# Half of each norm on VectorE, ranks from logits, a last sum by halves, and orders of smaller pieces in a small vision tower with a mixture of experts

## The reference

```
h = tok(x)
h = h + A(norm(h))     linear attention, elu features
h = h + B(norm(h))     softmax attention, qkv with 2 of 8 low-rank experts
h = h + C(norm(h))     attention with normed q and k, softmax over the queries; + its input
h = h + D(norm(h))     norm, softmax attention and a gelu MLP; second half of the batch with smaller branches
h = h + E(norm(h))     attention with a polynomial in place of exp
h = h + F(norm(h))     one int8 product
h = h + G(norm(h))     softmax attention, then a norm with gain and bias (G2)
h = h + H(norm(h))     2 of 8 experts (192 -> 768 gelu -> 192) by a softmax gate
```

## Time and profile before

| | us |
|---|---|
| median of three runs | 493.92 |
| lowest, highest of them | 493.78, 496.96 |
| the profiled execution, its time | 493.1 |
| its span, first to last instruction | 491.0 |
| TensorE busy | 434.6 |
| VectorE busy | 281.4 |
| ScalarE busy | 170.9 |
| GpSimd busy | 122.5 |

### The profile page before, as it was taken

How to read it: one execution, slowest core, us unless ns; L and a number is a source line. 1 busy time by engine, 2 the same in 40 slices (tenths; PEclk the granted TensorE clock), 3 DMA queues, 4 the chain that set the end, 5 groups by cost and what they waited for, 6 DMA issues and landing times.

```text
span 491.0 us, 11691 instructions
## 1 busy us (share of the span) xinstructions
PE 434.6 (89%) x4616; PEld 381.4 (78%) x4616; DVE 281.4 (57%) x862; ACT 170.9 (35%) x460; POOL 122.5 (25%) x169
## 2 busy tenths in 40 slices
PE   4999879999889889998999998989899779999990
PEld 4966767978578778787887887878889668999990
DVE  2367825858558894686346557698988451313111
ACT  0231022406051423553456431346332016354430
POOL 8120620102112003302021202430022175532230
PEclk9999959999999989999999998999998769999996
DMA  8647200000025000000000800101383113998003
GB/s 329 151 100 195 60 0 2 4 1 1 1 64 155 1 1 1 2 3 1 1 1 1 287 6 1 65 1 54 108 265 74 39 57 103 308 328 283 27 24 127
DMA packets 26320, 39.76 MB, mean 81 GB/s; under 512 B 5612, under 2 KB 17916, under 8 KB 26268
## 3 DMA queue, kind: packets, MB, share of 16 engines
q1 hardware_dynamic: 24348, 34.99, 23.4%
q0 software_dynamic: 1632, 3.34, 2.2%
q10 hardware_dynamic: 288, 0.70, 0.4%
HBM read 35.43 MB, written 3.59 MB: 79 GB/s over the span
## 4 chain that ended last, share of the span: by engine, by line
PE 58%; DVE 16%; SPq 9%; issue 5%; POOL 4%; ACT 4%; DMA 3%; POOLq 0%; DVEq 0%
PE bank L1574 8%; PE bank L1668 8%; PE bank L1691 7%; PE bank L1621 6%; PE bank L1918 3%; PE bank L1626 3%; PE bank L1930 3%; PE bank L1866 3%; PE bank L1583 2%; SPq L511 2%; ACT xn L809 2%; PE bank L1903 2%; PE bank L1639 2%; DVE stats L1019 2%; POOL rstd L670 1%
## 5 line engine op out<-in xcount | busy, mean ns | idle before, releaser
L1574 PE MATMUL bank<-constants 128*128 128x128 f32 x622 | 83.8, 287 | 0.0
L1574 PEld LDWEIGHTS bank<-constants 128*128 128x128 f32 x622 | 76.5, 199 | 4.9 <-issue 4.1
L670 POOL TENSOR_TENSOR rstd<-rstd_tmp,minus_half 101x4 f32<-101x4 f32 x20 | 20.3, 1016 | 198.3 <-DVE rstd_tmp L1029 198.2
L809 ACT ACTIVATE xn<-h,minus_mean_rstd,rstd 101x192 f32<-101x192 f32 x64 | 30.0, 559 | 40.8 <-POOL minus_mean_rstd L677 40.7
L1918 PEld LDWEIGHTS bank<-vblk,et 101*64 101x64 f32 (+1 forms) x960 | 29.4, 127 | 4.4 <-issue 4.2
L1918 PE MATMUL bank<-vblk,et 101*64 101x34 f32 (+1 forms) x960 | 30.4, 220 | 2.3 <-ACT et L937 2.1
L1621 PE MATMUL bank<-weights,nT 128*101 128x192 f32 (+2 forms) x128 | 28.7, 366 | 0.9 <-DVE vblk L1083 0.9
L790 POOL DMA_INDIRECT rows_y<-et,out_row x17 | 17.0, 1002 | 43.8 <-DVE et L1529 42.4
L1621 PEld LDWEIGHTS bank<-weights,nT 128*101 128x101 f32 x128 | 19.6, 175 | 6.6 <-issue 6.5
L1709 PE MATMUL bank<-weights,scores 128*101 128x192 f32 x96 | 18.4, 362 | 6.9 <-DMA scores<-in_patches 6.9
L1903 PEld LDWEIGHTS bank<-packing,scores 101*101 101x101 f32 x240 | 22.2, 169 | 2.1 <-issue 2.1
(11 more groups left out here) (343 smaller groups left out, 933.1 us busy)
## 6 DMA issues: line engine op xcount, KB each, us to landing
weights<-in_w SPq DMA_DIRECT2D x7, 576.0 KB, 4.9
weights<-in_w SPq DMA_DIRECT2D x7, 384.0 KB, 5.0
scores<-in_patches SPq DMA_DIRECT2D x4, 606.0 KB, 7.1
scores<-in_w SPq DMA_DIRECT2D x4, 576.0 KB, 6.2
...
```

The costliest lines, as they stand in the source:

```text
L670: link(g.tensor_tensor(rstd[0:ROWS, a], rtmp[0:ROWS, a], mhalf[0:ROWS, a], ALU.pow))
L809: ins = sc.activation(dst, src, ACT.Identity, scale=rstd[0:ROWS, r:r + 1], bias=nmr[0:ROWS, r:r + 1])
L1574: mm(PS[b][:, 0:128], ident, ident, start=True, stop=True)
```

## The change

- Norms: ScalarE normalises rows 2 and 3 of an oct's four, VectorE rows 0 and 1, at the start of its step T (or G2), as soon as the power is there (`root_ready`); it uses mean and root directly, so it doesn't wait for GpSimd's product. Whoever reads the result waits for both (`normalised`). `moments` signals the variance first and the mean after it (`mean_ready`); two of the four aggregations are made ahead of the second two pairs' statistics.
- H's gate: ranks are made from the logits, ahead of the maximum, with one comparison against a constant triangle of 0 and a tiny number in place of two.
- Last sum: both loads, the additions and the store go by two halves of the columns; SP stores the first, ScalarE's queue the second.
- Orders: phases may be cut into pieces (PE_PARTS, DVE_PARTS, ACT_PARTS), and the order strings go over the pieces. All four strings are new, and so is IDLE, with 297 fillers in place of 319. In A's O the products of the two groups are no longer interleaved, attention's O waits for half of the values and transposes only, and C's key statistics are aggregated piece by piece.

```diff
-IDLE = {('A', 'T', 0): 6, ('A', 'M', 0): 7, ('A', 'M', 0, 1): 3, ('A', 'O', 0): 1, ('A', 'M', 1): 1, ('A', 'M', 1, 1): 3, ('A', 'O', 1): 1, ('A', 'Z', 1): 9, ('B', 'T', 0): 1, ('B', 'G', 0): 1, ('B', 'H', 0, 1): 1, ('B', 'F', 0): 5, ('B', 'S', 0): 14, ('B', 'H', 1, 1): 1, ('B', 'P', 0): 1, ('B', 'S', 1): 14, ('B', 'Z', 1): 8, ('C', 'S', 0): 6, ('C', 'T', 1): 1, ('C', 'R', 1): 32, ('C', 'S', 1): 6, ('C', 'Z', 0): 1, ('C', 'P', 0): 1, ('C', 'O', 1): 16, ('C', 'Z', 1): 1, ('C', 'P', 1): 1, ('D', 'T', 0): 9, ('D', 'F', 0): 1, ('D', 'S', 0): 8, ('D', 'F', 1): 3, ('D', 'P', 0): 1, ('D', 'O', 1): 2, ('D2', 'P', 0): 2, ('D2', 'U', 1): 1, ('E', 'S', 0): 8, ('E', 'P', 0): 1, ('E', 'O', 1): 4, ('E', 'P', 1): 1, ('G', 'T', 0): 16, ('F', 'T', 1): 7, ('G', 'S', 0): 9, ('G', 'T', 1): 7, ('G', 'F', 1): 2, ('G', 'O', 1): 22, ('H', 'T', 0): 9, ('H', 'G', 0): 2, ('H', 'C', 0): 12, ('H', 'T', 1): 30, ('H', 'G', 1): 1, ('H', 'C', 1): 11, ('rows',): 8}
+IDLE = {('A', 'T', 0): 2, ('A', 'M', 0): 7, ('A', 'M', 0, 1): 3, ('A', 'T', 1): 2, ('A', 'Z', 0): 2, ('A', 'O', 1, 1): 5, ('B', 'H', 0, 1): 1, ('B', 'F', 0): 5, ('B', 'T', 1): 1, ('B', 'S', 0): 6, ('C', 'K', 0): 1, ('B', 'P', 1): 13, ('C', 'R', 0): 2, ('C', 'S', 0): 6, ('C', 'R', 1): 34, ('C', 'P', 0): 14, ('C', 'Z', 1): 1, ('C', 'P', 1): 1, ('D', 'T', 0): 8, ('D', 'F', 0): 1, ('D', 'S', 0): 8, ('D', 'S', 1): 7, ('D', 'Z', 1): 3, ('D2', 'P', 1): 3, ('E', 'F', 0): 1, ('E', 'T', 1): 4, ('E', 'F', 1): 1, ('E', 'Z', 1): 3, ('G', 'T', 0): 25, ('F', 'T', 1): 2, ('G', 'S', 0): 14, ('G', 'F', 1): 2, ('G', 'S', 1): 20, ('G', 'O', 1, 1): 15, ('H', 'G', 0): 1, ('H', 'C', 0): 13, ('H', 'T', 1): 44, ('H', 'G', 1): 1, ('H', 'C', 1): 7, ('rows',): 8}
...
-ORDER_PE = ("0100010101011001000100101001101101110001001111110001110000110101001101010011101001001010011010110101001101011011000111")
-ORDER_DVE = ("0100010101011000100101001001101011101001011011010110110001001100110100110101101001001100011011010101010101011010010111")
-ORDER_ACT = ("1000101010001100101000011010001111110001100110101101101010010100110101100110011010011100011000110101100100110100011111")
-ORDER_POOL = ("0100101000110010110011101000110011010110001010001100111100100010101110101010110001001001111011011010101011000001111011")
-
-
-def schedule(order):
-
-    steps, at = [], [0, 0]
+ORDER_PE = ("0011000000101101110101001010100100001010111111001100001000110011011101101111000101001001001101011110101010101100110010000100110101111010010100111000000111110110100111")
+ORDER_DVE = ("000101000010011011001011010011100100010100101000001101110010101111100001010001010000100011110101001011011111111011111001010100100100011011101100000101110011101001111010001101011010001011100001010010010111010110101001010101010100100110011001010010010111110101101111")
+ORDER_ACT = ("0010010010110100010111001011000100000000110101111111011010100001000010011010101011010011111111110001100000100001011111000111110101001001001111100111010000111001001000011111100100011011010100010100000101111011101010101111")
+ORDER_POOL = ("0100110100000100111001111001111000010011000100110110101100111010011001001101010001100111010101011001011011000101011101")
+
+
+PE_PARTS = {"tok": 2, "M": 2, "X": 4, "O": 2, "V": 2}
+DVE_PARTS = {'tok': 2, 'A.F': 2, 'M': 2, 'F': 2, 'S': 4, 'W': 2, 'X': 4, 'N': 4, 'O': 2, 'K': 4, 'R': 2, 'V': 2, 'P': 2, 'T': 2, 'F.T': 2}
+ACT_PARTS = {"T": 2, "A.F": 2, "S": 4, "X": 4, "O": 2, "R": 3, "U": 4}
+POOL_PARTS = {}
...
+def schedule(order, parts):
+
+    steps, at, whole = [], [0, 0], []
+    for n, ph in PHASES:
+        k = parts.get(n + "." + ph, parts.get(n if n == "tok" else ph, 1))
+        whole += [(n, ph, i, k) for i in range(k)]
     for q in map(int, order):
-        steps.append(PHASES[at[q]] + (q,))
+        steps.append(whole[at[q]] + (q,))
         at[q] += 1
-    assert at == [len(PHASES)] * 2
-    assert [q for n, p, q in steps if (n, p) == ("H", "C")] == [0, 1]
+    assert at == [len(whole)] * 2
+    assert [q for n, p, i, k, q in steps if (n, p) == ("H", "C")] == [0, 1]
     return steps
 
 
-PE_STEPS, DVE_STEPS, ACT_STEPS, POOL_STEPS = map(schedule, (ORDER_PE, ORDER_DVE, ORDER_ACT, ORDER_POOL))
+def section(items, i, k):
+
+    return items[len(items) * i // k:len(items) * (i + 1) // k]
...
+        halves = [slice(FLAT // 2 * x, FLAT // 2 * x + FLAT // 2) for x in range(2)]
...
+        mean_ready = Signal(sem("mean_ready"), [e for e in norms_by(DVE_STEPS) if e[0] != "Cqk"])
+        root_ready = Signal(sem("root_ready"), [e for e in norms_by(POOL_STEPS) if e[0] != "Cqk"])
         rstd_ready = Signal(sem("rstd_ready"), norms_by(POOL_STEPS))
-        xn_ready = Signal(sem("xn_ready"), norms)
+        xn_ready, xn_begun = Signal(sem("xn_ready"), norms(ACT_STEPS)), Signal(sem("xn_begun"), norms(DVE_STEPS))
...
+        def normalised(eng, n, q):
+
+            eng.wait_ge(*xn_begun.at((n, q)))
+            eng.wait_ge(*xn_ready.at((n, q)))
...
-            sp.dma_start(choice[0], flat_rows(rows_y[0:T])).then_inc(choice_loaded[0], 16)
+            for x in range(2):
+                sp.dma_start(choice[0][:, halves[x]], flat_rows(rows_y[0:T])[:, halves[x]]).then_inc(choice_loaded[0][x], 16)
             sp.wait_ge(summed, 2)
-            sp.dma_start(flat_rows(out), total_h).then_inc(stored, 16)
-            sp.wait_ge(stored, 16)
+            sp.dma_start(flat_rows(out)[:, halves[0]], total_h[:, halves[0]]).then_inc(stored, 16)
+            sp.wait_ge(stored, 32)
...
-                link(g.tensor_tensor(rstd[0:ROWS, a], rtmp[0:ROWS, a], mhalf[0:ROWS, a], ALU.pow))
+                root_of = g.tensor_tensor(rstd[0:ROWS, a], rtmp[0:ROWS, a], mhalf[0:ROWS, a], ALU.pow)
                 if n == "D":
 
+                    link(root_of)
                     link(g.tensor_tensor(rtmp[0:ROWS, a], mv[0:ROWS, a, 1], rstd[0:ROWS, a], ALU.mult))
                     link(g.tensor_tensor(rtmp[0:ROWS, a], rtmp[0:ROWS, a], rstd[0:ROWS, a], ALU.mult))
                     link(g.tensor_scalar(rtmp[0:ROWS, a], rtmp[0:ROWS, a], EPS, None, ALU.add))
-                    link(g.tensor_tensor(rst2[0:ROWS, a], rtmp[0:ROWS, a], mhalf[0:ROWS, a], ALU.pow))
+                    root_of = g.tensor_tensor(rst2[0:ROWS, a], rtmp[0:ROWS, a], mhalf[0:ROWS, a], ALU.pow)
+                root_of.then_inc(*root_ready.inc((n, q)))
+                pool.wait_ge(*root_ready.at((n, q)))
+                pool.wait_ge(*mean_ready.at((n, q)))
...
-                for p in range(P8):
+                for p in range(BY_DVE, P8):
...
-            act.dma_start(choice[1], rows_y[T:2 * T].rearrange("t d -> (t d)").rearrange("(a b) -> a b", a=128)).then_inc(choice_loaded[1], 16)
+            for x in range(2):
+                act.dma_start(choice[1][:, halves[x]],
+                              rows_y[T:2 * T].rearrange("t d -> (t d)").rearrange("(a b) -> a b", a=128)[:, halves[x]]).then_inc(choice_loaded[1][x], 16)
+            act.wait_ge(summed, 4)
+            act.dma_start(out.rearrange("t d -> (t d)").rearrange("(a b) -> a b", a=128)[:, halves[1]], total_h[:, halves[1]]).then_inc(stored, 16)
...
+                if c % 2:
+                    settle()
+                    aggregate(c - 1)
...
-                for p in range(P8 * q, P8 * q + P8):
-                    mark(v.bn_aggr(mv[0:ROWS, p], stats[0:ROWS, p]))
+                aggregate(2 * q + 1)
                 settle()
                 a = slice(P8 * q, P8 * q + P8)
-                mark(v.tensor_scalar(nmr[0:ROWS, a], mv[0:ROWS, a, 0], -1.0, None, ALU.mult))
                 v.tensor_scalar(rtmp[0:ROWS, a], mv[0:ROWS, a, 1], EPS, None, ALU.add).then_inc(*var_ready.inc((n, q)))
+                v.tensor_scalar(nmr[0:ROWS, a], mv[0:ROWS, a, 0], -1.0, None, ALU.mult).then_inc(*mean_ready.inc((n, q)))
...
+            def normalise(n, q):
+
+                dve.wait_ge(*root_ready.at((n, q)))
+                for p in range(BY_DVE):
+                    r = P8 * q + p
+                    src, dst = (yt[q][0:ROWS, p], x2[q][0:ROWS, p]) if n in ("D2", "G2") else (h[0:ROWS, r], xn[0:ROWS, r])
+                    ins = v.tensor_scalar(dst, src, mv[0:ROWS, r, 0:1], rstd[0:ROWS, r:r + 1], ALU.subtract, ALU.mult)
+                    if n == "D" or p < BY_DVE - 1:
+                        mark(ins)
+                if n == "D":
+                    settle()
+                    for p in range(BY_DVE):
+                        r = P8 * q + p
+                        ins = v.tensor_scalar(x2[q][0:ROWS, p], xn[0:ROWS, r], rst2[0:ROWS, r:r + 1], None, ALU.mult)
+                        if p < BY_DVE - 1:
+                            mark(ins)
+                ins.then_inc(*xn_begun.inc((n, q)))
...
+                if n == "H":
+                    whose = ahead_by[0:ROWS].rearrange("p (i j) -> p i j", j=NE).unsqueeze(1).broadcast_to([ROWS, P8, NE, NE])
+                    link(v.tensor_tensor(diff, lg.unsqueeze(2).broadcast_to([ROWS, P8, NE, NE]),
```

(49 more changed lines are left out.)

201 lines of the change are left out of this document (111 added, 90 removed).

## The result

Median of 20 runs each: 492.41 us (488.12 to 496.63) against 496.75 us (493.78 to 503.18) before, 4.3 us less. The ratio, which leaves out slow executions (those over 1.5% longer than the fastest of their kernel), is 0.993, 95% interval 0.9901 to 0.9959; by it the change is worth 3.5 us. The forecast was 485.3 for 493.92, a ratio of 0.983. The sign was right and the time lies in the range, but of the 8.6 us forecast only 3.5 came.

The account below looks back on a forecast made before the run. No one engine bounds the whole; TensorE does in D, VectorE from G to H. Terms -5.9 + 3.8 + 0 - 1.4 + 0.8 - 5.9 = -8.6 us on 493.1 give 484.5, as a median 485.3; range 475 to 495.

Parts of the forecast that it names:

- VectorE's rows cost nothing at D2: At D2 of oct 0, as at B0, VectorE idles, so its half of the norm adds no time: 0.
- three pairs: VectorE's two-row norm pieces from F to H, where it is the bound: six at 0.63 us, +3.8 us in all.
- Part 1: All norms, half on VectorE: eight norms on the chain gain 0.74 us each, -5.9; VectorE's own queue pays +3.8.
- the 0.2 us for meeting GpSimd: At each chain norm, VectorE's and GpSimd's work stretch each other: 0.2 us taken off the 0.94 gain.
- the port rival: Four of VectorE's new pairs meet a GpSimd row addition and lose 1.5 us each: 491.3 us, chance 0.06.
- VectorE's wait for the power: At six norms in B to E VectorE waits about 10 us for GpSimd's power, costed at nothing because it idles there.
- Part 2: H's ranks from logits: oct 1's norm behind routing +2.3, given back by copy, picks and filler; sum 0, ends -1 and +1.5.
- the walk: Stepping through the four new order strings with the timelines' durations, leaving out contention and hand-over jitter; its moves make -8.8 us.
- Part 3: Last sum by halves at the kernel's end: additions -1.0 and smaller last store -0.4, together -1.4 us.
- Part 4: New orders in A to E: A +0.8; B -0.5, C -2.0, D0 -2.9, D2 -2.1, E -1.3, these five taken at two thirds, -5.9.
- Clock: Rival: 10 us more work at the 1.2 GHz level, half of that time lost, some 4.5: 489.8 us, chance 0.09.
- orders give nothing: Rival: VectorE stays the bound and TensorE's saved filler returns as waiting: 491.2 us, chance 0.12.

Follow-up runs that it names:

- e9: Changed kernel with GpSimd's addition to h in D's P waiting for both halves of the D2 norm: 491.20 us, 0.9898 of the kernel before.
- e6: Changed kernel with oct 1's H norm whole on ScalarE and 35 fillers in place of 44 ahead of its transposes: 491.71 us, 0.9902 of the kernel before.
- e5: Changed kernel with nine fillers ahead of G's first O piece of oct 1: 491.38 us, 0.9896 of the kernel before.
- e14: Changed kernel with the edits of e5, e6 and e9 together: 484.67 us, 0.9774 of the kernel before.
- e10: Changed kernel with all four rows on ScalarE at six norms (B, C, D2, E of oct 1, D of both): 495.64 us, 1.0015 of the kernel before.

## Why the size was wrong

At one clock 3.8 us were gained of the 8.6 forecast. Three steps of the prediction failed: that VectorE's rows cost nothing at D2 (2.2 us by e9), that oct 1's H norm behind the routing costs nothing in sum (1.7 by e6), and that the new filler table loses no clock, for which the sum has no term (1.0 at one clock by e5). Mended together they give 5.3 (e14). The forecast's terms (part 4's moves at two thirds, as in its sum), set by stages from one norm's transposes to another's against the table under e6, in us against before (profiles at 0.957 before, 0.952 in e6, 0.958 in e14):

| | forecast | e6 | e14 |
|---|---|---|---|
| start to D oct 0 (B0, A, B, C, D0) | -3.5 | -1.9 | -1.9 |
| D oct 0 to E oct 1 (D2) | -2.1 | -0.1 | -2.2 |
| E oct 1 to G oct 1 (four norms, three pairs, E) | -1.9 | -2.0 | -2.0 |
| G oct 1 to H oct 0 (two norms, two pairs) | -0.2 | +2.0 | +0.6 |
| H oct 0 to the end (a pair, parts 2 and 3) | -0.8 | -2.1 | -1.1 |
| sum | -8.6 | -4.1 | -6.6 |

The mended D2 and the norms from E to G come out as forecast. What stays short in e14 lies mainly ahead of D's norm (1.6), and 0.8 between G and H. The mean gain of e14 is above that of its profile, and that it meets the forecast all the same is in part luck. Step by step:

- **Part 1, right but for one place.** Pieces of 0.98 and 0.67 and a norm on the chain 0.83 sooner (B0, G0, F1, G1) stand by the forecast's 0.93, 0.63 and 0.74. The step that failed is "VectorE's rows cost nothing where it idles (B0, D2 0)", and with it the 0.2 us for meeting GpSimd. At both D2 norms the pair meets a whole addition and grows by 1.5 us. That is the price of the port rival; I gave it 0.06 because I put the meetings where GpSimd adds bias rows behind a norm, and never looked at what GpSimd does beside D2's. The row was in the trace of before: the addition, at 230.40, stood 0.1 us behind the product there too, beside ScalarE's rows. Worth 2.2 us (e9). The rule cited there (the Trainium skill, SBUF — State Buffer, "SBUF: two separate sides") agrees: of VectorE's eight rows of D2 and G2 the median took 0.38 us, the longest 1.95.
- **VectorE's wait for the power, right.** Costed at nothing; forecast 10.2 us at six norms, measured 10.7 at nine, and e10 shows that the split is worth having at the six.
- **Part 2, at the wrong end of its bounds.** The parts were right: the pair ends behind the routing, and from H's transposes to the cumulative product it is 5.23 us in place of 7.45. But I took 0 where the ends were -1 and +1.5. From oct 0's transposes to oct 1's it takes 3.7 more, not 2.3, because the routing ends 1.4 later behind oct 0's transposes than the walk took it to (in e6 too: 17.0); so 3.7 - 2.2 = 1.5 is lost. e6 gives 1.7 back.
- **Part 3, right.** -1.2 for -1.4. The halves do land apart: on SP's queue 3.0 and 3.7 us after their issue, on ScalarE's 3.2 and 4.0, where the whole took 4.1 and 4.3. The rule that I cited from the Trainium skill (DMA: Bandwidth & Descriptors, "Rules for kernel authors") is about halves of the partitions, and these are halves of the columns. I also read from it that the halves land together, which it doesn't say: for two halves issued from one engine it has the same ring on each of the 16 DMA engines, and packet-interleaved rings only for two issuing engines.
- **Part 4, right in D0, not in C.** From C's last column norm to D's transposes it takes 8.7 us (186.34 to 195.02), forecast 8 to 9. But the column norms end 2 us later than before, not sooner (1.1 in e6, whose C of oct 1 begins with that of before, at 146.2). VectorE's timeline there (before: the earlier trace rows):

```profile
162.71 1.25 DVE L1491 TENSOR_SCALAR x_y<-x_y,rstd_qk,minus_mean_rstd_qk 101x192 f32<-101x192 f32 x4 [1.06 <-POOL minus_mean_rstd_qk L722]
...
171.93 3.07 DVE L1153 TENSOR_TENSOR vblk<-bank,wide_biases 37x192 f32<-37x192 f32 x8 [2.35 <-PE bank L1714]
```

 The idle time ahead of the key rows shrinks from 2.49 to 1.06, and a new one of 2.35 appears: VectorE now waits for TensorE's oct 1 values of W, which stand behind an O piece of oct 0 and oct 1's own scores. The walk followed VectorE's string and not TensorE's beside it. (It also passed over a second idle time in the trace of before, 0.66 us at 162.80.) So D begins 1.9 sooner in e6 and e14, not the 3.5 of the terms up to there; no run mends this.
- **Clock, wrongly seen as a rival of the change.** Both kernels' executions average 0.948 and 0.946, some 0.6 us apart. G's O (e5) is a fall that the new filler table brought; there the forecast said "so the like may be regained" and did not go from place to place. Another, near 99, stands in the profiles of the changed kernel and of e5, e6, e9 and e14 and not in that of before; it was not tried by itself. In turn the fall of before near 300 is gone.
- The rival "orders give nothing" would have given nearly the measured time (491.2), but its reason, VectorE as the bound, is not what was found: with three places mended the same orders give a gain of the forecast's size (e14).
